# Layer-1 attention passes of a pair share one step for their 256-query tile

## The reference

```
attn = einsum('bhnd,bhkd->bhnk', q, k) / temperature        # layer 0, q and k normalised
out  = einsum('bhnk,bhkd->bhnd', softmax(attn), v)
...
scores = scale * einsum('bhqd,bhkd->bhqk', q, k)            # layer 1, q and k with layernorm and rope
scores = where(tril(ones(S, S)), scores, -inf)
out = einsum('bhqk,bhkd->bhqd', softmax(scores), v)
```

## Time and profile before

| | us |
|---|---|
| median of 3 runs | 894.79 |
| lowest and highest | 892.99, 894.9 |
| the profiled execution | 892.65 |
| its span, first to last instruction | 890.9 |
| its attention steps, first to last exponential | 21.7 to 861.8 |
| mean granted TensorE clock | 0.994 |

### The profile page before, as it was taken

One profiled execution on the slowest core, in us unless ns is written; L12 is line 12 of the kernel. 1 busy time (PEld: TensorE's weight loads), 2 busy tenths in 40 slices (PEclk: granted clock), 3 DMA queues, 4 the chain that ended last, 5 costly groups with the idle time before them and its releaser, 6 DMA issues.

```text
span 890.9 us, 16698 instructions
## 1 busy us (share of the span) xinstructions
PE 839.0 (94%) x6268; PEld 303.7 (34%) x6268; DVE 577.8 (65%) x1604; ACT 790.0 (89%) x896; POOL 156.0 (18%) x352
## 2 busy tenths in 40 slices
PE   8999999999999899999999999999899998989995
PEld 3233323323323333333333332333333332343443
DVE  6264756867777777767852577655833487657557
ACT  4899999989989899998999899999999998979961
POOL 3000000100002400124100511022100443352210
PEclk9999999999999999999999999999999999999999
DMA  5754414116207411541341321422220230413000
GB/s 155 245 173 147 166 43 148 60 36 240 68 30 238 136 36 36 188 156 36 141 144 36 119 72 37 136 78 72 100 90 25 95 108 25 140 63 118 1 13 25
DMA packets 48565, 88.60 MB, mean 99 GB/s; under 512 B 5088, under 2 KB 14432, under 8 KB 48480
## 3 DMA queue, kind: packets, MB, share of 16 engines
q1 hardware_dynamic: 48000, 87.00, 29.0%
q10 hardware_dynamic: 480, 0.48, 0.2%
HBM read 51.03 MB, written 35.65 MB: 97 GB/s over the span
## 4 chain that ended last, share of the span: by engine, by line
PE 56%; DVE 25%; ACT 9%; issue 5%; DMA 2%; POOL 1%; SPq 1%; DVEq 0%; ACTq 0%; POOLq 0%
PE ps L857 27%; PE ps L836 15%; ACT probs L709 9%; PE ps L805 4%; PE ps L816 3%; PE ps L812 2%; PE ps L731 2%; PE ps L790 2%; DVE mid_sq L1060 1%; DMA q_st<-parts_scratch 1%; DVE sums_t L1106 1%; DVE mid_part L1255 1%; DVE mid_part L1256 1%; POOL probs L625 1%; DVE heads_t L1110 1%
## 5 line engine op out<-in xcount | busy, mean ns | idle before, releaser
L709 ACT ACTIVATE probs<-ps 128x1024 f32<-128x1024 f32 (+1 forms) x832 | 770.2, 1006 | 68.6 <-PE ps L857 32.4
L857 PE MATMUL ps<-probs,v_st 128*32 128x512 f32 (+3 forms) x3584 | 431.7, 561 | 7.9 <-POOL v_st L607 3.4
L836 PE MATMUL ps<-q_st,k_st 32*128 32x512 f32 (+3 forms) x1792 | 277.4, 464 | 12.6 <-ACT probs L709 8.5
L836 PEld LDWEIGHTS ps<-q_st,k_st 32*128 32x128 f32 x1792 | 123.2, 182 | 269.1 <-ACT probs L709 178.9
L625 POOL TENSOR_SCALAR_AFFINE_SELECT probs<-probs 128x256 f32<-128x256 f32 x256 | 112.4, 454 | 220.8 <-ACT probs L709 215.6
L857 PEld LDWEIGHTS ps<-probs,v_st 128*32 128x32 f32 x3584 | 74.5, 108 | 117.5 <-issue 87.9
L607 POOL COPY v_st<-v_all 128x256 f32<-128x256 f32 (+1 forms) x65 | 29.4, 455 | 347.1 <-PE ps L857 337.5
L1106 DVE STREAM_TRANSPOSE sums_t<-ps 128x512 f32<-128x512 f32 x32 | 22.9, 717 | 49.8 <-PE ps L857 48.7
L1240 DVE COPY mid_qkv<-ps 128x384 f32<-128x384 f32 x32 | 17.9, 558 | 39.0 <-PE ps L805 38.9
L1240 DVE COPY prep_qkv<-ps 128x384 f32<-128x384 f32 x24 | 13.3, 556 | 38.5 <-PE ps L805 38.0
L812 PE MATMUL ps<-yTp,w_hid 128*128 128x512 f32 x84 | 30.8, 448 | 1.8 <-DVE yTp L1222 0.9
(11 more groups left out here) (177 smaller groups left out, 659.7 us busy)
## 6 DMA issues: line engine op xcount, KB each, us to landing
k_st<-parts_scratch SPq DMA_DIRECT2D x47, 512.0 KB, 3.6
parts_scratch<-mid_part SPq DMA_DIRECT2D x36, 512.0 KB, 4.2
q_st<-parts_scratch SPq DMA_DIRECT2D x63, 256.0 KB, 4.0
parts_scratch<-prep_part SPq DMA_DIRECT2D x28, 512.0 KB, 4.2
k_st<-parts_scratch SPq DMA_DIRECT2D x16, 256.0 KB, 2.8
xT<-in_xT SPq DMA_DIRECT2D x8, 256.0 KB, 5.2
x_all<-in_x SPq DMA_DIRECT2D x8, 256.0 KB, 5.9
out<-yo SPq DMA_DIRECT2D x7, 256.0 KB, 2.3
```

Source lines behind the costliest of these rows:

```text
L709: nc.scalar.activation(probs[:, k % PS, :, 0:w], slot(k)[:, :, 0:w], ACT.Exp).then_inc(probs_ready, 1)
L836: last_ = mm(slot(k)[:, e, at:at + n], k_st[row, p % KB, kt * P:(kt + 1) * P], q_st[row, p % KB, lo:HALF], start=True, stop=not shifted)
L857: last_ = mm(acc[HR * h:HR * (h + 1), lo:HALF], v_st[:, p % VB, kt, h, :], probs[:, (2 * s + h // 2) % PS, h % 2, at:at + n], start=first ...
```

## The change

`pair_steps` (L57 of the changed kernel) makes the steps of a pair at once. In layer 1 the 256-query tiles of the two passes, which were two narrow steps, become one wide step at the end of the first pass and the start of the second: (a, 2) with (z, 2), or (a, 6) with (z, 6). A pair has 5 steps instead of 6 with qh 0, and 13 instead of 14 with qh 1, so there are 400 steps, all wide. A tile now carries its pass. So pass a's tile of 256 queries moves behind all its others, and pass z's stays near the start of z, ahead of its first tile instead of behind it. Waits that named the first step of the next pass name the last step of this one. The planner gets the new steps and lays the same 202 stages into 400 steps.

```diff
-def pass_steps(layer, qh):
-    kts = [(kt,) for kt in range(KT)]
-    if layer:
-        kts = [(0,), (6,), (1,), (5, 7), (2,), (4,), (3,)] if qh else [(0,), (2,), (1, 3)]
+def pair_steps(p):
+    layer, b, qh, g = PASSES[p]
+    a, z = p, p + 1
+    if not layer:
+        kts = [[(x, kt)] for x in (a, z) for kt in range(KT)]
+    elif qh:
+        one = lambda x: [[(x, 0)], [(x, 1)], [(x, 5), (x, 7)], [(x, 2)], [(x, 4)], [(x, 3)]]
+        kts = one(a) + [[(a, 6), (z, 6)]] + one(z)
+    else:
+        one = lambda x: [[(x, 0)], [(x, 1), (x, 3)]]
+        kts = one(a) + [[(a, 2), (z, 2)]] + one(z)
...
+HOLDS = [[s for s in range(NS) if p_ in [x[0] for x in STEPS[s][1]]] for p_ in range(NP)]
+FIRST, LAST_STEP = [x[0] for x in HOLDS], [x[-1] for x in HOLDS]
...
-                sp.wait_ge(scores_ready, 2 * FIRST[p - KB + 1])
+                sp.wait_ge(scores_ready, 2 * (LAST_STEP[p - KB] + 1))
...
-                pool.wait_ge(sums_ready, FIRST[p - VB + 1])
+                pool.wait_ge(sums_ready, LAST_STEP[p - VB] + 1)
...
         def scores(k, shifted):
-            p, tiles_, w, m, first, last = STEPS[k // 2]
-            if k % 2 == 0 and first:
-                pe.wait_ge(rows_in[p % KB], 32 * (p // KB + 1) + (32 * PRODUCTS - 32 if p % KB == 0 else 0))
...
+            s, tiles_ = k // 2, STEPS[k // 2][1]
+            for p in dict.fromkeys(x[0] for x in tiles_):
+                if k % 2 == 0 and FIRST[p] == s:
+                    pe.wait_ge(rows_in[p % KB], 32 * (p // KB + 1) + (32 * PRODUCTS - 32 if p % KB == 0 else 0))
...
         def sums(s):
-            if first:
-                pe.wait_ge(v_in, p + 1)
-                if p and p % 2 == 0:
-                    pe.wait_ge(sums_turned, p // 2)
+            for p in dict.fromkeys(x[0] for x in tiles_):
+                if FIRST[p] == s:
+                    pe.wait_ge(v_in, p + 1)
+                    if p and p % 2 == 0:
+                        pe.wait_ge(sums_turned, p // 2)
...
-            for x, (kt, lo, at, n) in enumerate(tiles_):
+            for x, (p, kt, lo, at, n) in enumerate(tiles_):
```

More of the change, by code:

```diff
@@ L67, in pass_steps @@
         tiles, at = [], 0
[L68 removed]
+        for x, kt in group:
             lo = max(kt * P - qh * HALF, 0) if layer else 0
[L70 removed]
+            tiles.append((x, kt, lo, at, HALF - lo))
             at += HALF - lo
[L72 removed]
+        out.append((tuple(tiles), at, layer == 1 and group[0][1] * P >= qh * HALF))
     return out
 STEPS = []
[L78 to L84 removed]
+for p_ in range(0, NP, 2):
+    for tiles_, w_, m_ in pair_steps(p_):
+        STEPS.append([tiles_[0][0], tiles_, w_, m_])
 NS = len(STEPS)
+HOLDS = [[s for s in range(NS) if p_ in [x[0] for x in STEPS[s][1]]] for p_ in range(NP)]
+FIRST, LAST_STEP = [x[0] for x in HOLDS], [x[-1] for x in HOLDS]
+STEPS = [(*x, FIRST[x[0]] == s, LAST_STEP[x[0]] == s) for s, x in enumerate(STEPS)]
 MASKED = [2 * sum(x[3] for x in STEPS[:s + 1]) for s in range(NS)]
[L87 removed]
 def passes_of(layer, c):
@@ L548, in _ @@
             parts = [slot_of(layer_job[layer], c, "qkT", 0) for c in range(chunks_needed(layer, b, qh))]
-            todo.append((max([first_slot(p - KB + 1) + 2 if p >= KB else 1] + [s + 1 for s in parts]), 3, "rows", p, None))
+            todo.append((max([LAST_STEP[p - KB] + 1 if p >= KB else 1] + [s + 1 for s in parts]), 3, "rows", p, None))
         todo += [(10 + 2 * c, 5, "x_all", c, None) for c in range(NCH)]
@@ L622, in mask @@
                 pool.wait_ge(probs_ready, k + 1)
-                for kt, lo, at, n in STEPS[s][1]:
+                for x, kt, lo, at, n in STEPS[s][1]:
                     block_ = probs[:, k % PS, :, at:at + P]
@@ L652, in _ @@
             got = [slot_of(layer_job[layer], c, "qkv", TC - 1) for c in range(chunks_needed(layer, b, qh))]
-            todo.append((max([FIRST[p - VB + 1] + 2 if p >= VB else 0] + [s + 1 for s in got]), 2, "load", p))
+            todo.append((max([LAST_STEP[p - VB] + 3 if p >= VB else 0] + [s + 1 for s in got]), 2, "load", p))
         for name in job:
@@ L831, in scores @@
                 pe.wait_ge(probs_ready, k - SLOTS + 1)
-            for kt, lo, at, n in tiles_:
+            for p, kt, lo, at, n in tiles_:
                 for e in range(2):
@@ L839, in scores @@
                         row = slice(h * HR, h * HR + PARTS)
-                        last_ = mm(slot(k)[:, e, at:at + n], ones_st[row, :], shift_st[row, lo:HALF], start=False, stop=True)
+                        last_ = mm(slot(k)[:, e, at:at + n], ones_st[row, :], shift_st[row, p % 2, lo:HALF], start=False, stop=True)
             last_.then_inc(scores_ready, 1)
         def sums(s):
-            p, tiles_, w, m, first, last = STEPS[s]
-            if first:
-                pe.wait_ge(v_in, p + 1)
-                if p and p % 2 == 0:
-                    pe.wait_ge(sums_turned, p // 2)
-            if p == 0 and tiles_[0][0] == TC:
+            _, tiles_, w, m, _, _ = STEPS[s]
+            for p in dict.fromkeys(x[0] for x in tiles_):
[3 more added lines that the diff above has]
+                        pe.wait_ge(sums_turned, p // 2)
+            if tiles_[0][0:2] == (0, TC):
                 pe.wait_ge(more_v_in, 1)
@@ L854, in sums @@
                 pe.wait_ge(probs_ready, 2 * s + 2)
-            for x, (kt, lo, at, n) in enumerate(tiles_):
+            for x, (p, kt, lo, at, n) in enumerate(tiles_):
                 for h in range(GH):
                     last_ = mm(acc[HR * h:HR * (h + 1), lo:HALF], v_st[:, p % VB, kt, h, :],
-                               probs[:, (2 * s + h // 2) % PS, h % 2, at:at + n], start=first and p % 2 == 0 and x == 0,
-                               stop=last and p % 2 == 1 and x == len(tiles_) - 1, skip_group_check=True)
+                               probs[:, (2 * s + h // 2) % PS, h % 2, at:at + n], start=FIRST[p] == s and p % 2 == 0 and x == 0,
+                               stop=LAST_STEP[p] == s and p % 2 == 1 and x == len(tiles_) - 1, skip_group_check=True)
             last_.then_inc(sums_ready, 1)
```

23 lines of the change are left out of this document (6 added, 17 removed).

## The result

Before: 894.01 us, median of 4 runs (892.99 to 894.9). After: **885.11 us**, median of 4 (881.12 to 887.11). The range forecast began at 862 and ended at 876, so the time lies outside it, on the slow side.

A forecast was written before the change was run, and what follows sets the result against it. Narrow steps were taken to bound it: ACT idles until the sums free a buffer, so two cost 3.46 to 3.72 us against 1.81 for one wide step. Terms summed to -26.1 from 892.65, plus 1.5: 868 us, range 862 to 876.

The forecast's parts named there:

- Steps, -27.2: 16 layer 1 pairs: one wide step replaces two narrow ones, saving 1.70 us each, -27.2 us in all.
- Stages, 0: The 202 stages in PE's steps: those following a stage go from 84 to 86, their price moves along, 0.
- rival B: PE takes over: about 10 stage-laden pairs lose 0.47 us (+4.7), late DVE adds +2; 874 to 875 us; 23%.
- Rows of pass 18, +1.7: PE's wait for pass 18's rows, loaded behind mid2's stores, grows by one step, from 1.0 to near 2.7 us.
- Rows of second passes, +0.7: Second passes with qh 0: loads covered by one to two us, except pass 60's, 0 to 2 us late; +0.7.
- POOL behind a copy of new v, 0: Masks queued behind copies of v: mid7's new place gives -1.6 us, mid4's gets +1.6, together 0.
- Two stages at a turn, +1.9: Turns where PE's next stage waits for DVE, costing ACT 1.86 us: one such place becomes two, +1.9 us.
- Closing part, -2.1: End of the kernel: DVE held 1.0 us by `ln_rs1` and about 1.1 us by left-over units; -2.1 us.
- Clock, -1.1: Clock dip at 501.63 to 513.70 us: fuller steps leave fewer PE waits, -1.1 us, or 0 if elsewhere.
- ACT's idle time released by the sums: Sign: ACT's idle time ended by the sums falls from 32.4 to about 8 to 12 us.
- ACT waited behind the masks: Sign of error: the prediction is wrong if ACT still waits behind the merged steps' masks; no size given.

The follow-up runs named there:

- neither cause: Both kernels with the sums ahead of the stage behind a turn and the causal masks left out: changed kernel 862.69 us, kernel before 882.55 us.
- the second: The changed kernel run again unaltered for a second profile: 884.9 us, ratio 0.9885 to the kernel before.
- The order: Sums put ahead of the stage in PE's queue in the step after a turn: changed kernel 876.54 us, kernel before 891.57 us.
- two tries to move units: Changed kernel, sums first, chunk 4's copy of v one place later, xqT due 0.2 us earlier for the planner, or 1.5 us: 876.15 and 875.62 us.

## Why the prediction was wrong

- **Steps, -27.2.** The mechanism and the price in a clean pair were right (1.65 in pair 50). But pairs 32, 40 and 48 gained 1.17 to 1.19. With neither cause acting the sixteen pairs gained 19.1 where I had 25.5 (with the +1.7 for pass 18): this term was oversized by about 6. That is from single profiles, with half clock in two pairs of the one before.
- **Stages, 0.** Wrong: a stage in pairs 32 and 48 cost nothing before and 0.47 us after. This is rival B's other term, at B's price of 0.47 a pair. Counting stages that follow each other didn't show it, and said nothing on whether a stage's input from DVE is ready.
- **Rows of pass 18, +1.7.** Right in size: pair 16 took 12.36 us before and after. PE's own wait grew from 0.79 us to 1.57, not to 2.7.
- **Rows of second passes, +0.7.** Pass 60's rows were waited for 0.35 us: less than allowed for.
- **POOL behind a copy of new v, 0.** Both halves happened, mid4's larger: ACT idled 1.86 us behind it in the first profile and 2.67 in the second, against 1.6, and moving the copy gave pair 26 back 3.2. mid7's is in pair 52: nothing waits behind its copy any more (744.76), but the pair gained 1.42 us in all where 1.65 + 1.6 were due; PE's wait of 1.03 us for `xqT` of mid7 is new in it.
- **Two stages at a turn, +1.9.** The mechanism was right and the count wrong. In layer 1 the places became three; at the third a stage waits for DVE behind the turn and half clock follows. Pair 56, rid of its place, gained 3.45. The order was worth 5 us of the change's gain (8.4 against 3.2).
- **Closing part, -2.1.** Right in kind, and larger: 2.9 were gained.
- **Clock, -1.1.** The dip went (pair 34 fell from 12.08 to 9.31 us), but it was scatter, and the clock as a whole fell: 0.991 before and 0.985 after by the median of all executions of the first group. "Fuller steps leave fewer such waits" holds for the waits for slots (PE's fell from 8.5 us to 2.7); new waits for DVE took their place.
- **The step that failed** is what the sum has for waits for DVE: nothing. Only rival B prices them, "if DVE, with 27 us less for the same 578 us, is late for two or three stages, +2 more". DVE was late, as B says, but the price was not 2: with the queue behind it and the half clock, about 9 of the 16 us missing are its and the queue's (the change is worth 19.9 us without the two causes, 10 to 11 with them). The other 6 are the oversized first term. The 578 us were taken as fixed; 18 of them (577.2 against 558.8) are there only because of the masks. They are nearly the same 18 or 19 in the kernel before (577.8 against 559.1), where the masks' presence cost 5 us, not 16.

Two things that the prediction had named as signs of its being wrong did appear: ACT's idle time released by the sums fell to 24.1 us and not to 8 to 12, and ACT waited behind the masks of pair 26. Why the same inflation costs three times as much after is argued, not shown by a run of its own: the narrow steps gave DVE slack. That the planner's costs are one cause more is open too; two tries to move units by them only shifted the wait.

## What to carry to other kernels

When steps become shorter, look at each engine that is *not* full for work that others wait for by place in a queue: list the stages whose inputs end within a step of their use, and price each miss with everything queued behind it, half clock included. Put the instruction that is ready ahead of the one that may wait; here that one line was worth nearly as much as the change. And the busy time of an engine is not a constant of the work: take it without its neighbour before you count on it.

## What the runs showed of the hardware

- `affine_select` on 128x256 in GpSimd slows VectorE's 128x4 instructions with two SBUF inputs from 0.16 to 0.33 us while it runs (302.43 to 306.45 in the first profile), and the 128x256 `TENSOR_TENSOR` of the turn from 425 to 601 ns by the median; one-input statistics (281 ns) and transpositions from PSUM (717 ns) keep their time.
- An idle time of 2.66 us in PE was followed by 7 us at 0.51 of the clock, one of 2.98 us by 3.5 us at 0.52, one of 1.47 us by full clock, and so was one of 2.21 us at 599.91 in the changed kernel without masks. The 2.11 us of pair 26 had full clock behind them in the first profile of the changed kernel (sums of 1.07 us, 1.00 in 427 to 431) and half clock in the second (1.90 us, 0.62 in 425 to 429.5): the same wait of the same kernel, and pair 26 took 1.2 us longer in the second. The wait for the rows of pass 18 was 1.57 us in the first profile, with full clock behind it, and 1.43 in the second, with 0.50 from 292.4 to 295.8. So in these traces the length of a wait alone does not tell whether the clock falls.
